# A two-layer graph network kernel: the normalised rows of its convolution stage made by GpSimd in place of the vector engine

## What is computed

```python
def _layernorm(x, axis=-1, eps=1e-5):
    m = jnp.mean(x, axis=axis, keepdims=True)
    v = jnp.var(x, axis=axis, keepdims=True)
    return (x - m) / jnp.sqrt(v + eps)

h = jnp.maximum(_layernorm(x, axis=-1), 0.0)
x = x + _L0_gnn_ref(h, adj, ...)
# in _L0_gnn_ref:
xc = jnp.transpose(x, (0, 2, 1))
h = jax.nn.relu(_bn(_conv1d(xc, conv1_w, 0), ...))
h = _bn(_conv1d(h, conv2_w, 8), ...)
x_conv = jnp.transpose(jax.nn.relu(h + xc), (0, 2, 1))
```

## Time and profile before

| | |
|---|---|
| median of three runs | 1956.99 us |
| profiled execution, its own time | 1950.57 us |
| its span, first to last instruction | 1948.8 us |
| TensorE matmul busy | 1835.8 us (94%) |
| vector engine busy | 1488.0 us (76%) |
| ScalarE busy | 776.3 us (40%) |
| GpSimd busy | 448.6 us (23%) |
| granted TensorE clock, mean | 0.983 of full speed |

### The profile page before, as it was taken

How to read it: one execution, slowest core, us unless ns; L and a number is a source line. 1 busy time by engine, 2 the same in 40 slices (tenths; PEclk the granted TensorE clock), 3 DMA queues, 4 the chain that set the end, 5 groups by cost and what they waited for, 6 DMA issues and landing times.

```text
span 1948.8 us, 36555 instructions
## 1 busy us (share of the span) xinstructions
PE 1835.8 (94%) x12498; PEld 1388.5 (71%) x12498; DVE 1488.0 (76%) x3314; ACT 776.3 (40%) x1432; POOL 448.6 (23%) x589
## 2 busy tenths in 40 slices
PE   3779999999948999999999999999999999999997
PEld 2566777744426887887887887787787787777875
DVE  5899999922246787787778777877877877877876
ACT  4654444442233333343333333333333333333441
POOL 4411111100022222222222222222222222222221
PEclk9899999999978999999999999999999999999998
DMA  5376675592252232232232222222322322322320
GB/s 209 126 260 233 231 254 198 176 346 104 103 173 95 78 99 74 80 98 71 81 98 71 89 89 71 91 87 71 96 82 71 96 82 71 96 82 71 96 83 17
DMA packets 163713, 229.03 MB, mean 118 GB/s; under 512 B 13420, under 2 KB 110563, under 8 KB 162906
## 3 DMA queue, kind: packets, MB, share of 16 engines
q1 hardware_dynamic: 163656, 228.29, 35.2%
HBM read 138.06 MB, written 90.18 MB: 117 GB/s over the span
## 4 chain that ended last, share of the span: by engine, by line
PE 68%; DVE 1%; ACT 0%; DMA 0%; POOL 0%; issue 0%; POOLq 0%; DVEq 0%
PE ps_rz L1301 27%; PE ps_n L1301 14%; PE ps_l L1301 13%; PE ps_b L1301 9%; PE ps_s L1261 3%; PE ps_d L1516 1%; PE ps_d L1310 1%; DMA rows<-spectra 0%; POOL conv_v L1283 0%; POOL conv_x L1278 0%; ACT conv_y L1272 0%; DVE out_sum L1568 0%; DVE out_sb L1572 0%; DVE update L1481 0%; DVE u_s L1551 0%
## 5 line engine op out<-in xcount | busy, mean ns | idle before, releaser
L892 PE MATMUL m_ps<-big 128*128 128x512 f16 (+1 forms) x1152 | 267.0, 375 | 5.2 <-DVE ysb L803 3.0
L1472 POOL TENSOR_TENSOR x_new<-xin,new 128x256 f32<-128x256 f32 x128 | 108.8, 850 | 684.9 <-ACT new L1465 684.9
L1447 ACT ACTIVATE tanh_rz<-sum_rz,w_scale 128x512 f32<-128x512 f32 x128 | 91.9, 718 | 318.1 <-DVE sum_rz L1438 318.1
L1301 PE MATMUL ps_rz<-w_ih,conv_t 128*128 128x512 f32 x768 | 216.1, 417 | 0.0
L1301 PE MATMUL ps_rz<-w_ih,nmp 128*128 128x512 f32 x768 | 205.2, 402 | 0.7 <-DVE nmp L1394 0.7
L892 PEld LDWEIGHTS m_ps<-big 128*128 128x128 f16 x1152 | 112.0, 98 | 109.2 <-DVE ysb L803 4.0
L1301 PE MATMUL ps_rz<-w_hh,ht 128*128 128x512 f16 x768 | 187.2, 380 | 0.0
L1301 PE MATMUL ps_l<-w_l,h2t 128*128 128x512 f16 x768 | 178.6, 383 | 1.4 <-DVE h2t L1528 1.4
L1301 PEld LDWEIGHTS ps_rz<-w_ih,conv_t 128*128 128x128 f32 x768 | 139.8, 189 | 32.1
L803 DVE SCALAR_TENSOR_TENSOR ysb<-m_ps,ysb 128x512 f16<-128x512 f32 x96 | 66.0, 689 | 117.4 <-ACT ysb L722 117.1
L1301 PEld LDWEIGHTS ps_rz<-w_ih,nmp 128*128 128x128 f32 x768 | 134.7, 188 | 28.4 <-DVE nmp L1394 0.9
(11 more groups left out here) (211 smaller groups left out, 3601.3 us busy)
## 6 DMA issues: line engine op xcount, KB each, us to landing
xin<-in_x SPq DMA_DIRECT2D x128, 256.0 KB, 2.9
spectra<-ysb SPq DMA_DIRECT2D x96, 256.0 KB, 2.0
rows<-spectra SPq DMA_DIRECT2D x64, 384.0 KB, 3.4
x_normed<-xhat SPq DMA_DIRECT2D x64, 256.0 KB, 3.4
h_turned<-ht SPq DMA_DIRECT2D x64, 256.0 KB, 2.6
adj_in<-in_adj SPq DMA_DIRECT2D x64, 256.0 KB, 3.6
ht<-h_turned SPq DMA_DIRECT2D x64, 256.0 KB, 3.2
xhat<-x_normed SPq DMA_DIRECT2D x64, 256.0 KB, 3.0
```

Of the source, the lines that this page charges most:

```text
L892: last = pe.matmul(dest, x_, w_, start=n == 0, stop=n == 11, skip_group_check=True)
L1301: last = pe.matmul(dest, stationary(dl), moving(wl), start=start and n == 0, stop=stop and n == 2, **kw)
L1447: act.activation(tanh_rz[:, i, :], sum_rz[:, i, :], ACT.Tanh, scale=w["scale"][:, 4:5]).then_inc(S["rz_tanh"], 1)
L1472: pool.tensor_tensor(x_new[:, i, :], xin[:, p, i, :], new[:, i, :], ALU.add).then_inc(S["x_new_done"], 1)
```

## The change

The two TENSOR_SCALAR of `normalise` leave the vector engine's list and enter GpSimd's, directly behind the inverse root of the same graph, with the same waits. TensorE's and SyncE's waits on `xhat_done` stay as they are; GpSimd now gives it. The vector engine gets a wait in `layer_stats`, so that it doesn't overwrite the mean of a graph that GpSimd still reads.

```diff
@@ gpsimd
+                def normalise(f):
+                    pool.wait_ge(rstd_done, f + 1)
+                    if f >= 2:
+                        pool.wait_ge(turned, f - 1)
+                        pool.wait_ge(xhat_stored[f % 2], 16 * (f // 2))
+                    for t in range(H):
+                        last = pool.tensor_scalar(xhat[:, f % 2, t, :], xin[:, f % 2, t, :], meanvar[:, f % 2, t, 0:1],
+                                                  rstd[:, f % 2, t:t + 1], ALU.subtract, ALU.mult)
+                    last.then_inc(xhat_done, 1)
+
                 layer_rstd(0)
+                normalise(0)
                 for q in range(graphs - 1):
                     layer_rstd(q + 1)
+                    normalise(q + 1)
@@ vector
                 def layer_stats(f):
                     dve.wait_ge(x_loaded[f % 2], 16 * (f // 2 + 1))
+                    if f >= 2:
+                        dve.wait_ge(xhat_done, f - 1)
...
-                def normalise(f):
-                    dve.wait_ge(rstd_done, f + 1)
-                    if f >= 2:
-                        dve.wait_ge(turned, f - 1)
-                        dve.wait_ge(xhat_stored[f % 2], 16 * (f // 2))
-                    for t in range(H):
-                        last = dve.tensor_scalar(xhat[:, f % 2, t, :], xin[:, f % 2, t, :], meanvar[:, f % 2, t, 0:1],
-                                                 rstd[:, f % 2, t:t + 1], ALU.subtract, ALU.mult)
-                    last.then_inc(xhat_done, 1)
...
                 layer_stats(0)
-                normalise(0)
...
                         add_bias(q - 1)
-                    if q + 1 < graphs:
-                        normalise(q + 1)
                     if 0 <= q - 1 < graphs:
                         split_h1(q - 1)
```

## The result

The changed kernel takes 1996.19 us (median of 4 runs) against 1955.22 (4 runs): ratio 1.0219, interval 1.0202 to 1.0236, 41 us slower. The forecast was 12 us slower, 1969, with a range from 1956 to 1990. The direction was right, the size was over three times too small, and the result lies above the range.

A forecast was written before the change was run, and what follows sets the result against it. The vector engine was taken to bound convolution slots without products, TensorE those with them. Late rows through GpSimd add 3.3 + 7.7 + 1.0 = 12 us, giving a median of 1969 us, range 1956 to 1990.

The forecast's parts named there:

- the two regimes: Convolution-stage slots: first without products of spectra, vector-engine-bound, 15 of 4.43 us; second with products, TensorE-bound, 44 of 4.94 us.
- the removal gains nothing: Vector engine, before the split of h1: the 0.7 us freed becomes a wait for ScalarE's ReLU, costed at nothing.
- the loops as written down: Convolution stage, statistics through GpSimd and TensorE back to statistics: 7.15 + N per two first-regime slots, 18.31 + N per four second-regime.
- The price of N: Time of the normalising pair on GpSimd including contention, taken as 2.15 us from the filter-row scaling.
- the forecast's two terms: Convolution-stage slots made slower by the late rows: 3.3 us in the first regime, 7.7 us in the second.
- the forecast's own band: The forecast case: GpSimd pair of 1.8 to 2.4 us, whole kernel 6 to 17 us more, chance 0.52.
- the loop with one pass: Second regime, four slots through GpSimd once: 18.31 + N, 20.46 us at 2.15, 5.115 a slot.
- the loop with two passes: Second regime, four slots through GpSimd twice: 16.08 + 2N, 20.38 us at 2.15, ruling above N = 2.23.
- The rival: Mutual exclusion of GpSimd's pair and the vector engine's split of h1: pair of 2.7 us, total 1984, chance 0.15.
- The start: First turn of the convolution stage: moves 1.4 us later, partly taken back by slow first slots; costed at 1.0 us.
- SyncE's loads: Loads of x released by xhat_done 1.2 to 1.4 us later, slack above 1 us; costed at nothing.
- each rival: Whole kernel: mutual exclusion 1984 (0.15), dear second step 1990 (0.11), not slower 1957 to 1958 (0.19), faster 1947 (0.03).

The follow-up runs named there:

- no_pair: Changed kernel with the normalising pair left out on every engine, a one-column GpSimd memset signalling instead: 1951.51 us, 0.9992 of the kernel before.
- writes_warm: Changed kernel with two GpSimd memsets replacing the pair and six unused TensorE products ahead of each of the first 18 turns: 1973.12 us, 1.0083 of the kernel before.
- warm: Changed kernel plus six unused 512-column TensorE products ahead of each turn in the 18 slots without products: 1985.08 us, 1.0164 of the kernel before.
- writes_only: Changed kernel with GpSimd's pair replaced by two memsets of about 1.2 us each that read nothing: 1986.09 us, 1.0161 of the kernel before.

## Why the prediction was right or wrong

- *What bounds the two regimes, and that the removal gains nothing.* Right, and shown by no_pair.
- *The mechanism.* Right: the rows come late through GpSimd, TensorE's turn waits for them in 34 of the turns, and the loops as written down give the bare slots within 0.04 us (writes_warm).
- *The price of N.* Wrong. The step that failed is "I take 2.0, the middle of the pairs, plus 0.15 for the second step and for contention". The length alone is 2.43, since the second step costs 0.22 us an instruction and the second scalar 0.07. By the loops, N = 2.43 makes 4.79 and 5.235 a slot, some 6 and 13 us, 8 more than the forecast's two terms. The sum had a slip as well: for N of 2.4, the end of the forecast's own band, it gives 17 us by the loop with one pass, where the loop with two passes, which it says takes over above 2.23, gives 18 to 19.
- *TensorE's clock.* Missing altogether. The prediction had TensorE idle more in the first regime and did not ask what idling does to it, although the rows of the stage's start showed it: four transposes took 1.09 us at 75.97 and 0.66 later. No term of the sum stood for it. The loop of the first regime runs through TensorE, so the slow convolution delays what TensorE waits for next. Measured by warm: 11 us, 12 in the stage.
- *Contention.* Half right as a rival, mis-sized in the forecast, which put it in the same 0.15 as the second step. The rival had the split of h1 and GpSimd's two instructions exclude each other whole, 0.9 us on every pair (2.7 against 1.84). A pair is lengthened by about 0.5 at most and a split by 0.13 (0.27 in warm), and it depends on where the split starts. Measured by writes_only: about 10 us, 12 in the stage, most of it in the second regime. The Trainium skill (SBUF — State Buffer, Who interferes with whom) says that a vector instruction with two SBUF inputs contends with a GpSimd instruction that reads SBUF and not with one that only writes. writes_only agrees. The Trainium skill (SBUF — State Buffer, Summary: rules for kernel authors) adds that the second to issue blocks until the first is done. The rows agree in that one waits for the other, but not for the whole instruction: the split of 271.96 starts 0.69 us into the pair's first instruction of 1.22 and takes its usual 0.69, while splits that start 0.12 to 0.36 us into the second (warm, the kernel after) all wait until 0.39 into it. Read so, GpSimd holds the vector engine off only in an early part of each instruction, and a split that is running when GpSimd's next instruction starts holds that off, by up to 0.5 us. This reading fits the rows; why it ends at 0.5 is not shown, and no run tried it by itself.
- *The start, SyncE's loads.* 1.8 us up to the first turn against 1.0; the loads cost nothing (0.6 us of waiting in all), as said.
- *The range* ended 33 us above the kernel before, at 1990, because each rival was priced alone. The truth was a longer N with contention on top and a third effect in none of them.

The sum in the end, 6 + 13 us worked out for the bare length, 11 measured for the clock and 10 for contention, is 40 against 41 measured. In the stage, where the traces separate them best, it is 19.3 for the bare length, 12.2 for the clock and 12.3 for contention: 43.8.

## What to carry to other kernels

Work taken off the busiest engine is worth nothing where it stood in that engine's own wait for another one: look at what the next instruction waits for before counting a gain. Where a change puts latency into a loop through TensorE, ask whether TensorE will then idle long enough to lose its clock, because the slow products stand in the same loop. When an instruction moves to GpSimd, price it by a row with the same number of arithmetic steps, and look for a vector instruction with two SBUF inputs that will run beside it.

## What was not expected of the hardware

- A GpSimd TENSOR_SCALAR of 128x256 F32 takes 0.93 us with one step and one scalar per row, 1.15 with a second step, 1.22 with a second scalar. The Trainium skill (GPSIMD Engine Reference, Engine selection) calls one-input operations roughly line-rate; here 40 columns fewer save 0.13 us, 3.3 ns a column, and the two halves take 2.43 us against the vector engine's 0.72.
- Six extra products a slot, 1.46 us of useless work for TensorE, make the first regime 0.7 us a slot faster.
- The hold-up between GpSimd and the vector engine depends on where the one starts within the other. A split started 0.69 us into the pair costs it 0.05, at 1.03 it costs 0.39, at 1.19 it costs 0.5; started at 1.34, 1.48 or 1.56, the split itself takes 0.27, 0.13 or 0.05 more and always ends 2.30 us after the pair's start.
- Two memsets on GpSimd went by their columns and not by their bytes: 1320 columns of BF16 take 1.2 us, 1024 of F32 take 0.95, 0.9 ns a column, about a quarter of the pair's 3.3. Other shapes may differ: a memset of 384 columns of BF16 in the same kernels takes 0.66 to 0.70.
